# Graph network block on one core: two-byte spread and four 32-row products in the scores, softmax shares through logarithms and PSUM, and record sends dealt out anew

## The reference, cut to what matters

```python
q = (x @ Wq + bq).reshape(n, H, C)          # H = 4 heads, C = 32
e = (edge_attr @ We).reshape(-1, H, C)      # 32 edge features per edge
kj = k[src] + e
vj = v[src] + e
alpha = jnp.einsum('ehc,ehc->eh', q[dst], kj) / np.sqrt(C)
amax = jax.ops.segment_max(alpha, dst, num_segments=n)
ex = jnp.exp(alpha - amax[dst])
denom = jax.ops.segment_sum(ex, dst, num_segments=n)
alpha = ex / (denom[dst] + 1e-16)
agg = jax.ops.segment_sum(vj * alpha[:, :, None], dst, num_segments=n)
```

## Time and profile before

| what | value |
|---|---|
| median of 3 runs | 5401.89 us (5398.77 to 5412.19) |
| span of the profiled execution | 4651.0 us, 50018 instructions |
| median less span | 750.9 us |
| busy in the span: POOL / PE / DVE / ACT | 3414.1 / 2871.3 / 2230.8 / 613.9 us |
| mean granted share of TensorE's clock | 0.754 |
| moved by DMA | 599.91 MB, 129 GB/s |

### The profile page before, as it was taken

One profiled execution on the slowest core, in us unless ns is written; L12 is line 12 of the kernel. 1 busy time (PEld: TensorE's weight loads), 2 busy tenths in 40 slices (PEclk: granted clock), 3 DMA queues, 4 the chain that ended last, 5 costly groups with the idle time before them and its releaser, 6 DMA issues. The chain is left out here.

```text
span 4651.0 us, 50018 instructions
## 1 busy us (share of the span) xinstructions
PE 2871.3 (62%) x13750; PEld 2210.0 (48%) x13751; DVE 2230.8 (48%) x2711; ACT 613.9 (13%) x1076; POOL 3414.1 (73%) x3213
## 2 busy tenths in 40 slices
PE   3799998967777777751989643444444333333333
PEld 1688887943333333331989433333333333333333
DVE  7899997656666666668971621111111111111112
ACT  0355554010000000001751000000000000000000
POOL 1888886857777777767867677777777777777775
PEclk8899999968877878875999866666666566555556
DMA  6466566816666666651989523222222122212221
GB/s 191 139 189 183 170 187 209 265 37 172 170 170 170 170 171 173 173 153 59 278 241 276 174 68 94 68 68 68 68 68 68 49 53 52 53 53 53 53 53 51
DMA packets 498663, 599.91 MB, mean 129 GB/s; under 512 B 190115, under 2 KB 367441, under 8 KB 496248
## 3 DMA queue, kind: packets, MB, share of 16 engines
q0 software_dynamic: 117856, 246.12, 19.4%
q1 hardware_dynamic: 337751, 229.77, 17.7%
q10 hardware_dynamic: 42944, 122.68, 7.3%
HBM read 406.69 MB, written 204.36 MB: 131 GB/s over the span
## 5 line engine op out<-in xcount | busy, mean ns | idle before, releaser
L1151 PE MATMUL ps<-got,g_hot 128*128 x3224 | 719.2, 414 | 1151.3 <-DMA got<-y_back,s_msg 597.5
L721 POOL DMA_INDIRECT rec_by_src<-rec,pos x782 | 1123.9, 1437 | 344.1 <-issue 245.8
L1151 PEld LDWEIGHTS ps<-got,g_hot 128*128 128x128 f32 x3224 | 667.8, 316 | 1213.1 <-issue 1213.1
L1612 POOL DMA_INDIRECT sc_kv<-kv,d_src x806 | 762.0, 945 | 254.9 <-issue 245.3
L1036 POOL DMA_INDIRECT got<-y_forward,d_msg x782 | 739.1, 945 | 238.2 <-issue 238.2
L1036 POOL DMA_INDIRECT got<-y_back,s_msg x766 | 722.7, 943 | 241.7 <-issue 233.1
L806 PE MATMUL ps<-ln_low,ln_hot 128*125 128x256 f32 x2848 | 618.9, 380 | 19.7 <-DVE ln_low L783 15.9
L806 PEld LDWEIGHTS ps<-ln_low,ln_hot 128*125 128x125 f32 x2848 | 535.3, 188 | 103.2 <-issue 22.7
L1059 DVE TENSOR_TENSOR g_hot<-ps,src_loc 128x1024 f32<-128x1024 f32 x101 | 123.4, 1224 | 832.1 <-PE ps L1151 831.7
L1715 PE MATMUL ps<-q,sc_hotT 128*128 x1616 | 274.2, 322 | 236.4 <-DVE sc_hotT L1657 207.4
L1067 DVE TENSOR_TENSOR g_y<-ps,ms_b 128x384 f32<-128x384 f32 x75 | 41.8, 558 | 732.1 <-PE ps L1164 732.1
(11 more groups left out here) (328 smaller groups left out, 3102.4 us busy)
## 6 DMA issues: line engine op xcount, KB each, us to landing
linked<-ln_out SPq DMA_DIRECT2D x320, 224.0 KB
ve<-sc_kve ACTq DMA_DIRECT2D x202, 256.0 KB
wv_ve<-ve SPq DMA_DIRECT2D x101, 512.0 KB, 5.0
l_links<-linked SPq DMA_DIRECT2D x25, 800.0 KB, 7.3
l_links<-linked ACTq DMA_DIRECT2D x25, 800.0 KB, 9.2
attr_pairs<-ln_feats POOLq DMA_DIRECT2D x7, 2048.0 KB
sc_attr<-attr_pairs SPq DMA_DIRECT2D x202, 64.0 KB, 2.6
sc_kv<-kv,d_src POOLq DMA_INDIRECT x806, 3.0
```

Source lines behind the costliest of these rows:

```text
L721: pool.indirect_dma_start(out=dram["rec_by_src"], out_offset=bass.IndirectOffsetOnAxis(ap=S["pos"][:, c:c + 1], axis=0), in_=S["rec"][:, c ...
L1151: last = pe.matmul(ps[:, bass.ds(columns[j], width)], hot[:, q, j, :], got[:, bass.ds(slots[j], width)], start=False, stop=True, skip_grou ...
L1612: pool.indirect_dma_start(out=kv[:, q, j, :], out_offset=None, in_=dram["kv"], in_offset=bass.IndirectOffsetOnAxis(ap=S["d_src"][:, c:c + ...
```

## The change

Five parts.

1. `index_stage`: a third store, `loc_two`, holds the local numbers in two bytes (a DVE cast into `two`, one DMA); the store of the front value of `node` moves here from `softmax_maxima`. POOL issues 10 sends ahead of its wait for `tiled`, and 6 behind the gathers, as before.
2. `scores`: the spread is a two-byte product (ones and `sc_locr` BF16). The features' product is four products of 32 rows each, one into each of PSUM banks 0 to 3 (`by_pair`), and has one buffer, so PE waits for `added` of the step before. Transpose and spread have one buffer each (`before` in place of `before_last`). The four loads of `softmax_maxima` are issued by SP at step 24 of this stage, into tiles that outlive it. In the last four steps `heat` is interleaved with `score`.
3. `softmax_maxima`: Exp writes to `mx_back`; for the shares ACT takes Ln of the sum plus 1e-16 (`mx_guard`), DVE subtracts, ACT takes Exp. The addition, the reciprocal and the product on DVE go.
4. `weigh_values`: once per round of 6 groups DVE copies the round's shares (4 x 48 columns) into PSUM (`hand`), and the multiplication reads them there.
5. `RECORD_PARTS` deals the 782 sends anew: index 6 to 16, m0 (`mlp_layer`) 30 to 38, maxima 82 to 16, weigh 100 to 138, l2 76 to 86; m1 42 and the rest stay.

```diff
-RECORD_PARTS = {"index": 6, "link": 302, "l0": 70, "m0": 30, "project": 22, "maxima": 82, "weigh": 100, "m1": 42, "l2": 76, "norm": 0}
+RECORD_PARTS = {"index": 16, "link": 302, "l0": 70, "m0": 38, "project": 22, "maxima": 16, "weigh": 138, "m1": 42, "l2": 86, "norm": 0}
...
+            if send is not None:
+                first, last = part_of(send)
+                send_some(pool, S, dram, first, last - LATER)
...
+                    sp.dma_start(dram["loc_two"].rearrange("(b p) e -> p b e", p=P), two[:, :].rearrange("p (b e) -> p b e", e=P)).then_inc(saved, 16)
...
+                        link(dve.tensor_copy(two[:, :], wide[:, n % 2, 0:s.cols]))
...
+        by_pair = ps[:, 0:STEP * BANK].rearrange("p (k c) -> p k c", c=BANK)[:, :, 0:D]
...
+        def before(eng, sems, q, i):
+            eng.wait_ge(sems[(q - 1) % WAYS], i + 1 + (q >= 1))
...
+                if n == 4 * WAYS:
+                    for name, a in (("before", dram["node"][0:rows]), ("node", dram["node"][1:1 + rows]), ("after", dram["node"][2:2 + rows]),
+                                    ("place", dram["loc"].rearrange("b e -> (b e)")[0:rows])):
+                        sp.dma_start(S["mx_" + name][:, :], a.rearrange("(p c) -> p c", p=P)).then_inc(S["noded"], 16)
...
-            for q in range(TAIL):
+            for q in range(min(2, TAIL)):
                 heat(WHOLE, q)
             for q in range(TAIL):
+                if q + 2 < TAIL:
+                    heat(WHOLE, q + 2)
                 score(WHOLE, q, WHOLE, size(WHOLE * WAYS + q))
...
-                before_last(pe, heated, q, i)
-                pe.matmul(spread_loc(q), S["ones"][0:1, :], locr[0:1, q, :], start=True, stop=True).then_inc(spread[q], 1)
+                before(pe, heated, q, i)
+                pe.matmul(spread_loc(q), one_row[:, :], locr[0:1, q, :], start=True, stop=True).then_inc(spread[q], 1)
...
-                pe.matmul(feat(q), attr_t[:, q % 2, :], S["w_e"][:, :], start=True, stop=True).then_inc(product[q], 1)
-
+                before(pe, added, q, i)
+                for j in range(STEP):
+                    own = slice(j * EDGE_DIM, (j + 1) * EDGE_DIM)
+                    last = pe.matmul(by_pair[:, j, :], attr_t[own, q % 2, :], S["w_e"][own, j * D:(j + 1) * D], start=True, stop=True)
+                last.then_inc(product[q], 1)
...
-                act.activation(score[:, h, :], score[:, h, :], ACT.Exp).then_inc(exped, 1)
+                act.activation(back[:, h, :], score[:, h, :], ACT.Exp).then_inc(exped, 1)
+            for h in range(HEADS):
+                act.wait_ge(summed, h + 1)
+                act.activation(back[:, h, :], back[:, h, :], ACT.Ln, bias=guard[:, 0:1]).then_inc(logged, 1)
+            for h in range(HEADS):
+                act.wait_ge(weighted, h + 1)
+                act.activation(score[:, h, :], score[:, h, :], ACT.Exp).then_inc(shared, 1)
...
-                link(dve.tensor_scalar_add(back[:, h, :], back[:, h, :], 1e-16))
-                link(dve.reciprocal(back[:, h, :], back[:, h, :]))
-                dve.tensor_tensor(score[:, h, :], score[:, h, :], back[:, h, :], ALU.mult).then_inc(shared, 1)
-            dve.wait_ge(shared, HEADS)
+                dve.engine_nop().then_inc(summed, 1)
+            for h in range(HEADS):
+                dve.wait_ge(logged, h + 1)
+                dve.tensor_tensor(score[:, h, :], score[:, h, :], back[:, h, :], ALU.subtract).then_inc(weighted, 1)
...
+        share = ps[:, 7 * BANK + P:7 * BANK + P + HEADS * WAYS * GROUP].rearrange("p (a c) -> p a c", a=HEADS)
...
+            def hand(i):
+                dve.wait_ge(weighed[WAYS - 1], i + 1)
+                dve.tensor_copy(share, S["alpha"][:, :, bass.ds(start_of(i, 0), WAYS * GROUP)]).then_inc(handed, 1)
+                dve.wait_ge(handed, i + 1)
```

More of the change, by code:

```diff
@@ L438, in index_stage @@
         wide = m.sb(tag + "_wide", [P, 2, widest])
+        two = m.sb(tag + "_two", [P, PAIR_COLS], BF16)
         below = m.sb(tag + "_below", [P, TILES])
+        front = m.sb(tag + "_front", [1, 1])
+        fronted, begun = m.sem(tag + "_fronted"), m.sem(tag + "_begun")
+        LATER = 6
         ready, spread, tiled, stepped, flipped, listed = (m.sem(tag + n) for n in (
@@ L471, in _ @@
             if send is not None:
-                send_records(pool, S, dram, send)
+                send_some(pool, S, dram, last - LATER, last)
         @block.sync
         def _(sp):
+            sp.wait_ge(fronted, 1)
+            sp.dma_start(dram["node"][0:1].rearrange("(a n) -> a n", a=1), front[:, :]).then_inc(begun, 16)
             for k, s in enumerate(stairs):
@@ L533, in climb_of @@
                 dve.engine_nop().then_inc(stepped, 1)
+            dve.memset(front[:, :], -1.0).then_inc(fronted, 1)
             dve.wait_ge(spread, 1)
@@ L1570, in scores @@
         attr_t = m.sb("sc_attrT", [P, 2, P])
-        locr = m.sb("sc_locr", [1, WAYS, STEP * P])
+        locr = m.sb("sc_locr", [1, WAYS, STEP * P], BF16)
+        one_row = m.sb("sc_ones", [1, P], BF16)
         hot_t = m.sb("sc_hotT", [P, WAYS, STEP * P])
@@ L1709, in step @@
                 pe.wait_ge(featured[q], (i + 1) * 16)
-                before_last(pe, kept, q, i)
+                before(pe, kept, q, i)
                 pe.transpose(turn(q), attr[:, q, :], S["ident"][:, :]).then_inc(turned[q], 1)
@@ L1744, in softmax_maxima @@
         turn = m.sb("mx_turn", [P, HR, P])
-        node = m.sb("mx_node", [P, L])
-        node_b = m.sb("mx_before", [P, L])
-        node_a = m.sb("mx_after", [P, L])
-        loc = m.sb("mx_loc", [P, L])
+        node, node_b, node_a, loc = (S["mx_" + name] for name in ("node", "before", "after", "place"))
         bad = m.sb("mx_bad", [P, L])
@@ L1759, in softmax_maxima @@
         into = m.sb("mx_into", [P, HEADS])
-        front = m.sb("mx_front", [1, 1])
         turned, kept, stored, loaded, order, asked, told, ready, exped, shared, done = (m.sem("mx_" + n) for n in (
             "turned", "kept", "stored", "loaded", "order", "asked", "told", "ready", "exped", "shared", "done"))
-        fronted, noded = m.sem("mx_fronted"), m.sem("mx_noded")
+        summed, logged, weighted = (m.sem("mx_" + n) for n in ("summed", "logged", "weighted"))
+        guard = m.sb("mx_guard", [P, 1])
         divided, refilled = ([m.sem(f"mx_{n}{h}") for h in range(HEADS)] for n in ("divided", "refilled"))
@@ L1814, in _ @@
         def _(sp):
-            sp.wait_ge(fronted, 1)
-            sp.dma_start(dram["node"][0:1].rearrange("(a n) -> a n", a=1), front[:, :]).then_inc(stored, 16)
-            sp.wait_ge(stored, 16)
-            for t, a in ((node_b, dram["node"][0:P * L]), (node, dram["node"][1:1 + P * L]),
-                         (node_a, dram["node"][2:2 + P * L]), (loc, flat_loc[0:P * L])):
-                sp.dma_start(t[:, :], a.rearrange("(p c) -> p c", p=P)).then_inc(noded, 16)
             for h in range(HEADS):
@@ L1824, in _ @@
                              turn[:, h * PAIR_BLOCKS:(h + 1) * PAIR_BLOCKS, :]).then_inc(stored, 16)
-            sp.wait_ge(stored, 16 * (1 + HEADS))
+            sp.wait_ge(stored, 16 * HEADS)
             for h in range(HEADS):
@@ L1838, in _ @@
             link = Chain(dve, order)
-            dve.memset(front[:, :], -1.0).then_inc(fronted, 1)
-            dve.wait_ge(noded, 16 * 4)
+            dve.wait_ge(S["noded"], 16 * 4)
+            link(dve.memset(guard[:, :], 1e-16))
             link(dve.tensor_scalar(bad[:, :], loc[:, :], 0.0, None, ALU.is_lt))
@@ L1901, in _ @@
             dve.wait_ge(exped, HEADS)
-            carried(2, False, same, score, top, 0.0, ALU.mult, ALU.add)
+            carried(2, False, same, back, top, 0.0, ALU.mult, ALU.add)
             for h in range(HEADS):
@@ L1975, in group @@
                 ve4 = ve[:, q].rearrange("p k (a c) -> p k a c", c=HEAD)
-                dve.tensor_tensor(ve4, ve4, S["alpha"][:, :, cols].rearrange("p a k -> p k a")
+                dve.tensor_tensor(ve4, ve4, share[:, :, q * GROUP:(q + 1) * GROUP].rearrange("p a k -> p k a")
                                   .unsqueeze(3).to_broadcast([P, GROUP, HEADS, HEAD]), ALU.mult).then_inc(weighed[q], 1)
             with dve.Fori(0, WHOLE) as i:
+                hand(i)
                 for q in range(WAYS):
                     group(i, q)
+            hand(WHOLE)
             for q in range(REST):
@@ L2233, in gnn_kernel @@
         "attr_pairs": scratch("attr_pairs", [PAIR_COLS, P, EDGE_DIM]),
-        "linked": scratch("linked", [2, WINDOWS, KEYS, P]), "loc": scratch("loc", [PAIR_COLS, P]),
+        "linked": scratch("linked", [2, WINDOWS, KEYS, P]), "loc": scratch("loc", [PAIR_COLS, P]), "loc_two": scratch("loc_two", [PAIR_COLS, P], BF16),
         "node": scratch("node", [PAIR_COLS * P + P]), "src_firsts": scratch("src_firsts", [TILES]), "kv": scratch("kv", [ROWS, 2 * D]),
@@ L2286, in gnn_kernel @@
             S["alpha"] = a.sb("alpha_cols", [P, HEADS, PAIR_COLS])
```

(3 more changed lines are left out.)

29 lines of the change are left out of this document (16 added, 13 removed).

## The result

The changed kernel took 5638.16 us (median of 4 runs, 5631.44 to 5643.84), the kernel before beside it 5401.58 (4 runs, 5398.77 to 5412.19): a ratio of 1.0426, 95% interval 1.0408 to 1.0444. The forecast was 5384.5, its range ended at 5412.

A forecast was written before the change was run, and what follows sets the result against it. Bounds were read by stage: POOL's gathers in scores, DVE with PE close in weigh, a DVE chain with transfers in maxima. Terms 2 + 0 - 6 - 6.5 - 21 + 6.5 + 7.6 = -17.4 gave 5384.5 us, range 5364 to 5412.

The forecast's parts named there:

- carry the 750.9 over unchanged: Whole kernel: unprofiled median 5401.9 exceeds the profile's span of 4651.0 by 750.9 us, added unchanged to the forecast.
- Weigh, +6.5: Weigh: copying shares to PSUM stops DVE once per round, +6.5 us, bounds 4 and 12.
- hidden: Weigh: with shares in PSUM, 138 sends at 1.27 take 176 us, inside a stage of 210, costing nothing.
- Index, +2: Index stage: ten more sends fit POOL's idle time; the third store costs 2 us, bounds 0 and 4.
- Scores, -6: End of scores: interleaved heat and one-pass spread let the last step finish sooner, -6 us, bounds 0 and -7.
- the new loop of scores passes 5.0: Scores, rival (8%): the step exceeds POOL's 5.0 us; scores grows by 40, kernel at 5424.
- circle: Scores: one-buffer loop of product (1.91), spread, heat, addition and hand-over, 4.6 to 5.1 us at the low clock.
- Maxima, -6.5 and -21: Maxima: earlier loads save 6.5 us at the front; Ln and subtraction replacing the reciprocal save 21 at the end.
- Table load: End of maxima: table load taken as 1.28 us; the skill's 2.66 would make this term 1.4 smaller.
- m1 and l2, +7.6: Linked sum: ten more sends make POOL end last, the stage 7.6 us later, bounds 0 and +8.
- m0, 0: m0: eight more sends take 10.2 us within POOL's 15.12 us idle before project, costing 0.
- Shares in PSUM don't free POOL (5%): Weigh, rival (5%): 138 sends stay at 1.82, taking 251 us against a stage of 210: +41, so 5425.

The follow-up runs named there:

- e5: The changed kernel again, unedited, on a chip of the quick group (A): 4648.13 us beside 4655.76 for the kernel before, ratio 0.9986.
- e1: The kernel before again, no edit, for a second profile, on a chip of the quick group (A): 4655.62 us, span 4653.9.
- e7: The kernel before, no edit, profiled on a chip of the slow group (B): 5403.98 us, span 5402.2.
- e3: The changed kernel with only the features' product taken back to one product of 128 rows with two banks: 4643.23 us, ratio 0.9967.
- e13: e3 with one bank for the product instead of two, on a chip of the quick group (A): 4648.95 us.
- e2: The changed kernel with the function scores as before, the four moved loads kept in it: 4649.52 us, ratio 0.9982.
- e6: The kernel before, no edit, on the same chip as e5: 4658.93 us.
- e9: e3 with the weights left in SBUF, no copy per round in weigh: 5431.51 us, ratio 1.0043.
- e15: The changed kernel with 128x512 POOL writes behind sends after l0, and one product in one bank: 5327.42 us beside 5417.24 for the kernel before.
- e19: The changed kernel with one product in two banks, 128x128 POOL writes behind sends after l0 except in maxima, new send table: 5284.03 us, ratio 0.9763.
- e8: The changed kernel with the old table of sends (82 in maxima, 100 in weigh): 5598.57 us, ratio 1.0353.
- e10: The kernel before with the new scores' four products, but the spread in four bytes: 5472.58 us, ratio 1.0116.
- e12: The changed kernel with a POOL write behind each send after l0 and each gather of scores, on a quick chip (A): 5055.48 us.

## Why the prediction was wrong

By its own steps, with what e5 and e1 show on chips A and the changed kernel and e7 on chips B:

- *"So I work on the span and carry the 750.9 over unchanged."* This step failed, and the others that missed were read from rows that it made to stand for another chip. The 751 us were not around the program but in its stages: on a chip B scores is 268 us longer, linked sum 140, norm 42, the gathers 263. A sum made against rows of a 4651 us execution did not carry over to runs of 5402. The parts of the miss, in spans on B: weigh's term 175 us, scores' 58, m0's 11, linked sum's 5.
- *Weigh, +6.5.* +181.9 on B, +14.2 on A. The reasoning on the mechanism was right: with the weights in PSUM a send takes 957 ns. Its use was the fault: "hidden" supposed that PE and POOL do not hinder each other. On B, 138 sends 1.26 us apart let PE make 55 records in 152 us, and the stage took 384 us instead of 210. The earlier trace rows had such a place, sends of 0.97 in linked sum, but of a chip on which they hinder nobody. On A the 17 copies came to 6.1 us busy and 4.5 idle ahead of them; e3, with the same copies, has weigh at 211.8, so the last 4 us of e5's 216.3 can't be placed (e13, with the same weigh, has 215.4, e2 210.0).
- *Index, +2.* The stage after it starts 1.7 us later on A (e5 against e6, one chip) and 0.3 on B: within its bounds.
- *Scores, -6.* On A -4.9 against e1, -6.6 against e6. On B +52.1, by the four products (e9, e15 to e19 against e8 and the changed kernel). The rival "the new loop of scores passes 5.0" gave the right sign with the wrong mechanism: its circle is not what binds (e10, e15). Its product was oversized too: the four take 0.81 us at the low clock in e5, not 1.91.
- *Maxima, -6.5 and -21.* -28.1 and -28.7: right on both groups. L1888 begins 17.7 us into the stage, 17 forecast.
- *Table load.* The row in maxima is 1.28 us and the next Exp starts 0.02 behind it: the dearer figure that the prediction cites from the Trainium skill is not seen here.

```profile
2507.96 4.30 ACT L1835 ACTIVATE mx_back<-mx_back,mx_guard 128x816 f32<-128x816 f32 x4 [25.79 <-DVEq L1936]
2512.27 1.28 ACT L1838 ACT_TABLE_LOAD   x1
2513.57 1.66 ACT L1838 ACTIVATE mx_score<-mx_score 128x816 f32<-128x816 f32 x2
```

- *m1 and l2, +7.6.* On A linked sum's DVE part ends at 2547.5 and norm begins at 2556.2, 8.7 later, where before 0.6 passed: +8.1 by POOL's last sends, as forecast. On B +12.4, ten sends at 1.26.
- *m0, 0.* 0 on A; on B +10.9, eight sends at 1.26.
- *Shares in PSUM don't free POOL (5%).* They did; the rival that was missing is "they free POOL, and that starves PE".

The sum of -17.4 stood against -9.7 (e1) or -13.0 (e6, the same chip) in spans and -7.6 in medians on chips A. There the forecast would have been a little too good; on the chip that was measured it was wrong by 254 us.

What stays open: whether the groups are kinds of chips or conditions that they were in; why unspaced issues of POOL starve PE in one of them (on all chips B the page lists scores' gathers without the landing times that it has in most profiles of chips A, so the records too are thinner there; whether recording and starving have one cause wasn't tried, as every run shown was recorded). Why the starving begins only behind l0: link and l0 have sends of 1.7 and 2.0 us, which fits, but was not varied. And whether the four products cost their 52 to 72 us by the number of PE's instructions (3636 against 2424 in scores), by the lower clock or by the change of tiling.

## What to carry to other kernels

Compare the span of the profile that you reason from with the times to be predicted before anything else; if they differ by more than a few us (here 1.7 lie around the span, 4653.9 against 4655.62 in e1), the profile is of another condition, and a stage's bound read from it may not be the bound there. An engine that issues transfers back to back can be worse than one that is held up: freeing it needs a look at what runs beside it, on the slowest chip that counts. On chips B a pause of half a microsecond between sends was worth far more than it cost; on a chip A the same pauses cost 141 us (e12) and gave nothing, so such a version needs a time on both.

## What the runs showed of the hardware that was not expected

- The same program takes 4656 to 4659 us on some chips and 5402 to 5417 on others (medians; single runs lie within 1% of each other on a chip).
- On the latter, sends 1.26 us apart let PE issue a weight load and its matrix instruction in 2.8 us; 1.78 apart they cost it nothing; 1.50 apart, half as much in weigh and a tenth in linked sum.
- The starving begins some 15 us into the sends and outlasts the last one by some 16 us, 13 of them without a DMA packet.
- With four 32-row products the granted clock stays at 0.50 (1.2 GHz) through scores on both groups of chips, though PE is busy for 705 of 1019 us; with one product of 128 rows it was 0.80 and 0.76 (e15), between the levels of 1.2 and 2.4 GHz. On a chip A this cost nothing.
